# Mixing matmuls as two 64x64 tiles of four blocks in place of four 32x32 tiles of two, with homes of 13 tiles in eleven regions

## The chip, the cores and the metric

The kernel runs on one core of one Trainium2 chip. The metric is device time in microseconds (us); a version's time is the median of its runs. Names of engines: PE is TensorE (PEld its weight loads), DVE VectorE, ACT ScalarE, POOL GpSimd, SP SyncE, which here only issues DMAs.

## The reference, cut to what matters

The input x has shape (1, 16, 1024, 1024): 16 channels, 1024 rows t, 1024 columns s, all float32 (64 MiB in, 64 MiB out). Two layers follow each other.

```python
# layer 0: a bias that depends on the distance row - column, through a small MLP
rel = tril(row - column);  pos = max(rel.max(-1), threshold)
nd  = log(|c*rel| + 1) / (log(|c*pos| + 1) + 1e-6)
h   = relu(nd * W1 + b1)                 # 32 hidden units per (row, column)
x   = x + (h @ W2 + b2)                  # 16 channels
# layer 1: mixing of the 16 channels, with weights of the row and weights of the column
ret  = einsum('MTS,MN->NTS', x, w + eye)
ret += rank-2 mixing with qw1[t], qw2[t]  +  rank-2 mixing with kw1[s], kw2[s]
ret += x * qdd[t]  +  x * kdd[s]
```

Layer 1 is thus, at each point, a 16x16 matrix of its row, A[t], plus a 16x16 matrix of its column, B[s], both applied to the 16 channels of y = x + bias.

## The kernel before, in words

**Layout.** The 1024 columns are cut into 8 blocks of 128. The 128 partitions hold 16 channels of 8 blocks, so that one 128x1024 tile in SBUF is 8 rows t of the whole picture (each partition: 8 rows of one channel of one block). There are 128 such tiles of rows. `GS` blocks share a group of partitions; before, GS is 2, so there are `GROUPS` = 4 groups of `GP` = 32 partitions.

**Mixing.** A row's matrix A[t] must be applied to 16 channels of each block of a group at once, so the weights of a group are a GP x GP matrix that holds the 16x16 matrix GS times on its diagonal and zeros elsewhere. PE's array is used as independent square tiles on its diagonal, one for each group: four of 32x32. A row step (`a_rows`, L732) does one tile of 8 rows: for each of 8 rows and each group one matmul of 128 columns, that is 32 matmuls; float32 makes each of them two weight loads and two matmuls in the trace, 64 of each. A column step (`b_columns`, L743) does 8 columns of a block: per column and group one matmul over all rows of a region (REGION_TILES x 8, 120 as a rule), again 64 loads and 64 matmuls. Its 16 steps cover the 128 columns of all blocks.

**Weights.** The matrices are made once and lie in DRAM as `a_mats` and `b_mats`. `mats_b` (all columns, GS x 16 x 128 floats per partition) is loaded once over zeros. For the rows SP loads chunks of 32 rows into `mats_in` (`load_mats_a`, L325, one DMA per group), and POOL spreads 16 rows at a time into `mats_a` (`spread_unit`, L428), multiplying by a mask `own_block` that leaves the values of a partition's own block and zeros in the others: an output of 128 x (16 x GS x 16). `mats_a` holds two such units.

**Regions and homes.** The 128 row tiles are cut into regions, 8 tiles and then eight times 15. SBUF holds three homes of 15 tiles (60 KB per partition each). In region k one home holds y of the region, a second takes the column mixing of the region (`take_b`: ACT L517 and DVE L629 copy it out of PSUM in turn), to which DVE adds the row mixing (`finish_tile`, L639) and from which it is stored; the third receives x of region k+1, to which the bias is added in place. The bias is added one slot behind where x lies.

**Order.** It is written out by hand, the same on every engine. In region k come 16 column steps, then one row step per tile. Between them, at the steps that `bias_step` names (as a rule every second one), comes a bias tile of region k+1: POOL multiplies the table of logarithms by the row scales (`hidden`, L451), ACT applies the relu (L490), PE multiplies by W2 into `bias` (L757, 128x64 weights, columns 512 wide), DVE and ACT (L657, L501) add the result to x. For the first 64 tiles of rows half the columns have a constant bias, so that one `hidden` per tile is enough; the last 64 need two. `hidden` has three buffers, the PSUM tensor `main` two, `bias` two.

**DMAs.** Loads of x (L317) and the stores (L268) go in pieces of 1 to 4 tiles, 8 DMAs each (one per block, 16 partitions, runs of 512 bytes). SP issues all loads, the loads of `mats_in` and half of the stores; ACT issues the other half. Each queue is in order. A load into a home waits for the store of the tiles that lay there (`load_x`). The pieces 0, 1 and 2 of region k+2 are issued in the row steps 7, 10 and 13 of region k, the rest at the start of region k+1, the last piece in its row step 6.

Of the kernel before, what the change touches and what calls it, by code (L numbers as in the profile page):

```python
# [9 lines left out]
S = 1024  # L10
W = 128
BLOCKS = S // W
GS = 2
GROUPS = BLOCKS // GS
GP = H * GS
HID = 32
# [2 lines left out]
COLS = ROWS * W  # L19
COL_TILES = W // ROWS  # L20
BANK = 512
REGION_TILES = (8,) + (15,) * 8
REGIONS = len(REGION_TILES)
FIRST_TILE = [sum(REGION_TILES[:k]) for k in range(REGIONS)]
ALL_TILES = S // ROWS
HALF_TILES = ALL_TILES // 2
HOME_TILES = max(REGION_TILES)
HOMES = 3
STORE_PIECES = {8: (2, 3, 3), 15: (2, 3, 3, 3, 4)}
LAST_STORES = (2, 3, 3, 3, 2, 1, 1)  # L30
LOAD_PIECES = {8: (1, 3, 4), 15: (1, 3, 3, 3, 4, 1)}
PORTIONS = (2, 2)
CHUNK = 32
CHUNK_TILES = CHUNK // ROWS
# [4 lines left out]
UNITS = S // UNIT  # L39
A_UNIT = H * GS * UNIT  # L40
RING = 3
# [12 lines left out]
def build(nc, x, W1, b1, W2, b2, c, L_mult, init_L, qw1, qw2, kw1, kw2, qdd, kdd, w, out):  # L54
# [6 lines left out]
    with ExitStack() as ctx:  # L61
# [3 lines left out]
        def sem(name):  # L65
            return ctx.enter_context(nc.semaphore(name))
# [4 lines left out]
        homes = sb("homes", [P, HOMES * HOME_TILES * COLS])  # L71
        mats_b = sb("mats_b", [P, GS * H * W])

        mats_in = sb("mats_in", [P, A_RING * H * CHUNK])
        mats_a = sb("mats_a", [P, 2 * A_UNIT])
        own_block = sb("own_block", [P, GS])
        hidden = sb("hidden", [P, RING, COLS])
# [61 lines left out]
        y_const_ready = sem("y_const_ready")  # L140
        main_ready = sem("main_ready")
        main_taken = [sem(f"main_taken{i}") for i in range(2)]
        out_done = [sem(f"out_done{i}") for i in range(len(LAST_STORES))]

        def tile_of(k, T):
            return FIRST_TILE[k] + T
# [30 lines left out]
        def bias_step(k, T):  # L177

            return 1 + T * (COL_TILES + REGION_TILES[k] - 3) // (REGION_TILES[k + 1] - 1)

# [34 lines left out]
            return sum(i < len(pieces(r)) for r in range(k + 1))  # L215

        def store_pieces(k):
            return LAST_STORES if k == REGIONS - 1 else STORE_PIECES[REGION_TILES[k]]

        def load_pieces(k):  # L220
            return LOAD_PIECES[REGION_TILES[k]]

# [35 lines left out]
        def of_block(tensor, pitch, b, offset, dims):  # L258
            start = (b // GS) * GP + b % GS
            return bass.AP(tensor, start * pitch + offset, [[GS * pitch, H]] + dims)  # L260
# [38 lines left out]
        def _(sp):  # L299
# [73 lines left out]
            loaded = [3, 5] + [0] * (REGIONS - 2)  # L373
            for k in range(REGIONS):

                while k + 1 < REGIONS and loaded[k + 1] < 5:
                    load_x(k + 1, loaded[k + 1])
                    loaded[k + 1] += 1
                if k == 2:
                    sp.wait_ge(scales_out, DMA)  # L380
                    sp.wait_ge(nd_ready, PART // 2 // ROWS)
                    sp.dma_start(row_scale[:, 0:PART // 2], late_scales[:, 0:PART // 2]).then_inc(scales_in, DMA)
                if k == 4:
                    sp.wait_ge(nd_ready, PART // ROWS)
                    sp.dma_start(row_scale[:, PART // 2:], late_scales[:, PART // 2:]).then_inc(scales_in, DMA)
                for T in range(REGION_TILES[k]):
                    v = chunk_behind(tile_of(k, T))
                    if v is not None:
                        load_mats_a(v)
                    if k + 1 < REGIONS and T == min(6, REGION_TILES[k] - 4):  # L390
                        load_x(k + 1, 5)
                    for i in range(len(store_pieces(k))):
                        if T == piece_start(store_pieces(k), i + 1) - 1 - (i == 4 and k < REGIONS - 1):
                            store_upper(k, i)
                    if k + 2 < REGIONS and T in (7, 10, 13):
                        load_x(k + 2, loaded[k + 2])
                        loaded[k + 2] += 1
            for i in range(len(out_done)):
# [407 lines left out]
```

## Time and profile before

| | us |
|---|---|
| median of 3 runs | 914.26 |
| lowest and highest run | 906.75, 917.98 |
| profiled execution, span from first to last instruction | 930.2 |
| PE busy with matmuls | 741.4 (80%) |
| DVE, POOL, ACT busy | 452.3, 432.9, 387.6 |
| HBM bytes read, written | 77.61 MB, 69.47 MB |

The profiled execution is one execution; the page gives its span and no separate time. Busy time of PE is taken from modelled ends of pipelined matmuls. DMA share is the mean share of the time in which the 16 DMA engines had a packet under way.

### The profile page before, as it was taken

To read this page: it belongs to the slowest core of one execution; us is meant where nothing else is said; L and a number is where in the kernel's file an instruction comes from. 1 tells how busy PE (TensorE), PEld (TensorE's weight loads), DVE (VectorE), ACT (ScalarE), POOL (GpSimd) and SP (SyncE) were. 2 spreads that over 40 slices of the span, in tenths; PEclk is the share of its full clock that TensorE was granted. 3 is DMA by queue.
4 is the path that set the end of the run, shared out by engine and by line. 5 is a ranking of instruction groups with operands and counts; after the bars stand their busy time and mean duration, and the time that the engine had idled before them with its cause. 6 is when DMAs were issued, how large, how long until landed. Compare 5 with 4: busy or idle time off the path is not lost. (4 is left out here: it accounts for less than half of the span.)

```text
span 930.2 us, 39085 instructions
## 1 busy us (share of the span) xinstructions
PE 741.4 (80%) x18210; PEld 547.7 (59%) x18210; DVE 452.3 (49%) x483; ACT 387.6 (42%) x412; POOL 432.9 (47%) x267
## 2 busy tenths in 40 slices
PE   0678864798678876898799978999689878897984
PEld 0255654576556655666557745677357645676974
DVE  7496522376345533564346524464336524464352
ACT  3958624553463435543433334344233342341200
POOL 3545421254233432365458745586358753581020
PEclk9888887999999999999999999999899988999997
DMA  6787687658975999587976898488875988589068
GB/s 132 183 172 140 147 180 167 145 100 190 194 180 125 183 184 201 124 183 161 223 156 129 174 181 192 94 172 172 182 162 110 199 178 151 106 176 227 5 155 200
DMA packets 301055, 149.63 MB, mean 161 GB/s; under 512 B 30045, under 2 KB 296669, under 8 KB 300893
## 3 DMA queue, kind: packets, MB, share of 16 engines
q1 hardware_dynamic: 231456, 113.56, 56.9%
q10 hardware_dynamic: 69436, 33.58, 17.0%
q8 instruction: 143, 2.34, 1.1%
q14 instruction: 20, 0.16, 0.1%
HBM read 77.61 MB, written 69.47 MB: 158 GB/s over the span
## 5 line engine op out<-in xcount | busy, mean ns | idle before, releaser
L451 POOL TENSOR_TENSOR hidden<-log_table,row_scale 128x1024 f32<-128x1024 f32 x192 | 365.4, 1917 | 367.4 <-PE bias L757 359.5
L743 PE MATMUL main<-homes,mats_b 32*32 32x120 f32 (+1 forms) x9216 | 286.5, 272 | 119.6 <-issue 83.3
L743 PEld LDWEIGHTS main<-homes,mats_b 32*32 32x32 f32 x9216 | 257.9, 133 | 187.5 <-issue 136.1
L490 ACT ACTIVATE hidden<-hidden,b_col 128x1024 f32<-128x1024 f32 x192 | 220.3, 1149 | 310.3 <-POOL hidden L451 205.1
L732 PEld LDWEIGHTS main<-homes,mats_a 32*32 32x32 f32 x8192 | 238.1, 129 | 78.6 <-issue 54.9
L732 PE MATMUL main<-homes,mats_a 32*32 32x128 f32 x8192 | 258.8, 275 | 23.7 <-issue 23.6
L657 DVE SCALAR_TENSOR_TENSOR homes<-bias,b_col,homes 64x512 f32<-64x512 f32 (+1 forms) x256 | 185.8, 747 | 174.9 <-DMA homes<-in_x 106.5
L757 PE MATMUL bias<-hidden,w_blocks 128*64 128x512 f32 x768 | 207.6, 648 | 17.7 <-DVE b_col L620 8.8
L639 DVE TENSOR_TENSOR homes<-main,homes 128x1024 f32<-128x1024 f32 x128 | 156.8, 1225 | 107.7 <-PE main L732 104.6
L629 DVE COPY homes<-main 128x960 f32<-128x960 f32 x64 | 74.1, 1157 | 179.7 <-PE main L743 179.5
L517 ACT ACTIVATE homes<-main 128x960 f32<-128x960 f32 (+1 forms) x80 | 71.1, 891 | 109.4 <-PE main L743 99.3
L428 POOL TENSOR_TENSOR mats_a<-mats_in,own_block 128x512 f32<-128x512 f32 x64 | 66.5, 1040 | 107.4 <-PE main L732 96.7
L501 ACT ACTIVATE homes<-homes,b_col 64x512 f32<-64x512 f32 x128 | 89.4, 749 | 64.5 <-DMA homes<-in_x 54.1
L757 PEld LDWEIGHTS bias<-hidden,w_blocks 128*64 128x64 f32 x768 | 46.4, 143 | 86.6 <-issue 74.6
L697 PE MATMUL bias<-relu_b,w_blocks 128*64 128x1 f32 x2 | 0.3, 241 | 15.1 <-DVE w_blocks L614 15.1
L290 DVE TENSOR_TENSOR homes<-homes 128x2048 f32<-128x2048 f32 x4 | 10.6, 2698 | 0.1
L697 PEld LDWEIGHTS bias<-relu_b,w_blocks 128*64 128x64 f32 x2 | 0.3, 204 | 15.1 <-issue 15.1
L691 PE MATMUL main<-homes 128*128 128x128 f32 x32 | 6.5, 389 | 3.0 <-DVE homes L594 3.0
L691 PEld LDWEIGHTS main<-homes 128*128 128x128 f32 x32 | 5.9, 206 | 4.8 <-DVE homes L594 3.2
L589 DVE TENSOR_TENSOR homes<-homes 128x2048 f32<-128x2048 f32 x2 | 6.2, 3110 | 0.1
L509 ACT ACTIVATE homes<-main 128x1024 f32<-128x1024 f32 x4 | 4.1, 1025 | 2.1 <-PE main L691 2.1
L473 ACT ACT_TABLE_LOAD x1 | 1.3, 1283 | 7.5 <-issue 7.5
(37 smaller groups left out, 32.2 us busy)
## 6 DMA issues: line engine op xcount, KB each, us to landing
homes<-in_x SPq DMA_DIRECT2D x200, 192.0 KB, 6.5
out_mixed<-homes ACTq DMA_DIRECT2D x104, 192.0 KB, 5.9
out_mixed<-homes SPq DMA_DIRECT2D x104, 192.0 KB, 5.6
homes<-in_x SPq DMA_DIRECT2D x72, 256.0 KB, 7.1
homes<-in_x SPq DMA_DIRECT2D x136, 64.0 KB
mats_in<-a_mats SPq DMA_DIRECT2D x128, 64.0 KB
out_mixed<-homes ACTq DMA_DIRECT2D x28, 256.0 KB, 8.0
out_mixed<-homes SPq DMA_DIRECT2D x28, 256.0 KB, 5.8
```

The costliest lines, as they stand in the source:

```text
L428: nc.gpsimd.tensor_tensor(mats_a[:, w % 2 * A_UNIT:(w % 2 + 1) * A_UNIT].rearrange("p (n b e) -> p n b e", n=H, b=GS), rows.unsqueeze(2).t ...
L451: nc.gpsimd.tensor_tensor(hidden_tile(u, g).rearrange("p (j s) -> p j s", j=ROWS), bass.AP(logs.tensor, logs.offset, [list(logs.ap[0]), [1 ...
L490: nc.scalar.activation(hidden_tile(u, g), hidden_tile(u, g), ACT.Relu, bias=b1_col[:, 0:1])\
L501: add = nc.scalar.activation(y_rows(high_half, k, T, b), x_rows(high_half, k, T, b), ACT.Identity, bias=b2_col[high_half, 1:2])
L517: nc.scalar.activation(mixed_columns(k, C), column_sums(k, C), ACT.Copy)\
L629: dve.tensor_copy(mixed_columns(k, C), column_sums(k, C)).then_inc(main_taken[b_tile(k, C) % 2], 1)
L639: dve.tensor_tensor(at, main[:, i % 2, :], at, ALU.add).then_inc(main_taken[i % 2], 1)
L657: add = dve.scalar_tensor_tensor(out=y_rows(rows, k, T, b), in0=falling(u, b, 0 if both else b * (P // 2), P if both else P // 2), scalar= ...
L691: mm = pe.transpose(main[:, i % 2, b * P:(b + 1) * P], comp[part][:, at:at + P], ident)
L732: mm = pe.matmul(main[of_group(g), i % 2, j * W:(j + 1) * W], a_weights(g, w, part * ROWS + j), y_row(k, T, g, j), start=True, stop=True)
L743: mm = pe.matmul(main[of_group(g), i % 2, j * W:j * W + REGION_TILES[k] * ROWS], b_weights(g, C * ROWS + j), y_column(k, g, C * ROWS + j), ...
L757: mm = pe.matmul(bias[into, u % 2, b * BANK:(b + 1) * BANK], w2_blocks[:, g, :], rows, start=True, stop=True)
```

## The change

`GS` becomes 4: a group is four blocks on 64 partitions, and the weights are 64x64 with four 16x16 matrices on the diagonal. There are two groups, so two tiles of 64x64 in the array. `mats_b` grows from 16 to 32 KB per partition, `mats_a` from 4 to 8 KB; for this the homes shrink from 15 to 13 tiles (180 to 156 KB for three), and the regions become 6, nine times 13, and 5 tiles. The pieces of loads and stores, the steps at which SP loads ahead, and the regions at which the late scales are loaded are adapted.

```diff
--- before.py
+++ after.py
@@ -10,7 +10,7 @@
 S = 1024
 W = 128
 BLOCKS = S // W
-GS = 2
+GS = 4
 GROUPS = BLOCKS // GS
 GP = H * GS
 HID = 32
@@ -19,16 +19,17 @@
 COLS = ROWS * W
 COL_TILES = W // ROWS
 BANK = 512
-REGION_TILES = (8,) + (15,) * 8
+REGION_TILES = (6,) + (13,) * 9 + (5,)
 REGIONS = len(REGION_TILES)
 FIRST_TILE = [sum(REGION_TILES[:k]) for k in range(REGIONS)]
 ALL_TILES = S // ROWS
 HALF_TILES = ALL_TILES // 2
 HOME_TILES = max(REGION_TILES)
 HOMES = 3
-STORE_PIECES = {8: (2, 3, 3), 15: (2, 3, 3, 3, 4)}
-LAST_STORES = (2, 3, 3, 3, 2, 1, 1)
-LOAD_PIECES = {8: (1, 3, 4), 15: (1, 3, 3, 3, 4, 1)}
+STORE_PIECES = {6: (2, 2, 2), 13: (2, 3, 3, 3, 2), 5: (2, 1, 1, 1)}
+STORE_SEMS = max(len(sizes) for sizes in STORE_PIECES.values())
+LOAD_PIECES = {6: (1, 2, 3), 13: (1, 3, 3, 3, 2, 1), 5: (1, 4)}
+AHEAD = (7, 10, 12)
 PORTIONS = (2, 2)
 CHUNK = 32
 CHUNK_TILES = CHUNK // ROWS
@@ -140,7 +141,7 @@
         y_const_ready = sem("y_const_ready")
         main_ready = sem("main_ready")
         main_taken = [sem(f"main_taken{i}") for i in range(2)]
-        out_done = [sem(f"out_done{i}") for i in range(len(LAST_STORES))]
+        out_done = [sem(f"out_done{i}") for i in range(STORE_SEMS)]
 
         def tile_of(k, T):
             return FIRST_TILE[k] + T
@@ -215,7 +216,7 @@
             return sum(i < len(pieces(r)) for r in range(k + 1))
 
         def store_pieces(k):
-            return LAST_STORES if k == REGIONS - 1 else STORE_PIECES[REGION_TILES[k]]
+            return STORE_PIECES[REGION_TILES[k]]
 
         def load_pieces(k):
             return LOAD_PIECES[REGION_TILES[k]]
@@ -373,26 +374,27 @@
             loaded = [3, 5] + [0] * (REGIONS - 2)
             for k in range(REGIONS):
 
-                while k + 1 < REGIONS and loaded[k + 1] < 5:
+                while k + 1 < REGIONS and loaded[k + 1] < min(5, len(load_pieces(k + 1))):
                     load_x(k + 1, loaded[k + 1])
                     loaded[k + 1] += 1
-                if k == 2:
+                if k == 3:
                     sp.wait_ge(scales_out, DMA)
                     sp.wait_ge(nd_ready, PART // 2 // ROWS)
                     sp.dma_start(row_scale[:, 0:PART // 2], late_scales[:, 0:PART // 2]).then_inc(scales_in, DMA)
-                if k == 4:
+                if k == 5:
                     sp.wait_ge(nd_ready, PART // ROWS)
                     sp.dma_start(row_scale[:, PART // 2:], late_scales[:, PART // 2:]).then_inc(scales_in, DMA)
                 for T in range(REGION_TILES[k]):
                     v = chunk_behind(tile_of(k, T))
                     if v is not None:
                         load_mats_a(v)
-                    if k + 1 < REGIONS and T == min(6, REGION_TILES[k] - 4):
+                    if k + 1 < REGIONS and len(load_pieces(k + 1)) > 5 and T == min(6, REGION_TILES[k] - 4):
                         load_x(k + 1, 5)
                     for i in range(len(store_pieces(k))):
                         if T == piece_start(store_pieces(k), i + 1) - 1 - (i == 4 and k < REGIONS - 1):
                             store_upper(k, i)
-                    if k + 2 < REGIONS and T in (7, 10, 13):
+                    if k + 2 < REGIONS and (T in AHEAD or k == 0 and T == REGION_TILES[0] - 1) \
+                            and loaded[k + 2] < len(load_pieces(k + 2)):
                         load_x(k + 2, loaded[k + 2])
                         loaded[k + 2] += 1
             for i in range(len(out_done)):
```

## Rows read from the trace of the kernel before

**Rows 1.** The page: PE's total; the instruction DMA queue; DMA packets.
```profile
PE 741.4 (80%) x18210; PEld 547.7 (59%) x18210; DVE 452.3 (49%) x483; ACT 387.6 (42%) x412; POOL 432.9 (47%) x267
...
DMA packets 301055, 149.63 MB, mean 161 GB/s; under 512 B 30045, under 2 KB 296669, under 8 KB 300893
...
q8 instruction: 143, 2.34, 1.1%
```

**Rows 2.** Waits of PE: line, what ended them, us, times, longest.
```profile
PE main L743 <- issue: 83.3, 45, 4.7
PE main L732 <- issue: 23.6, 17, 2.8
PE main L743 <- ACT homes L517: 19.7, 6, 8.6
```

**Rows 3.** Timeline, PE, last region, rows: start, us, what, [idle before, releaser].
```profile
894.95 3.94 PE L732 MATMUL main<-homes,mats_a 32*32 32x128 f32 x127 [1.40 <-issue]
...
905.36 3.85 PE L732 MATMUL main<-homes,mats_a 32*32 32x128 f32 x127 [1.11 <-issue]
912.05 5.45 PE L732 MATMUL main<-homes,mats_a 32*32 32x128 f32 x127 [2.85 <-issue]
918.28 2.28 PE L732 MATMUL main<-homes,mats_a 32*32 32x128 f32 x72 [0.78 <-issue]
```

**Rows 4.** Timeline, PE: undisturbed step pairs and bias tiles, three stretches.
```profile
257.43 1.08 PE L757 MATMUL bias<-hidden,w_blocks 128*64 128x512 f32 x4
258.44 3.59 PE L743 MATMUL main<-homes,mats_b 32*32 32x120 f32 x128
261.96 1.08 PE L757 MATMUL bias<-hidden,w_blocks 128*64 128x512 f32 x4
...
293.34 3.85 PE L732 MATMUL main<-homes,mats_a 32*32 32x128 f32 x128
297.13 1.08 PE L757 MATMUL bias<-hidden,w_blocks 128*64 128x512 f32 x4
...
605.35 3.85 PE L732 MATMUL main<-homes,mats_a 32*32 32x128 f32 x128
609.14 1.94 PE L757 MATMUL bias<-hidden,w_blocks 128*64 128x512 f32 x8
611.01 1.25 PE L732 MATMUL main<-homes,mats_a 32*32 32x128 f32 x36
```

**Rows 5.** Timeline, weight loads of one column step of the first region.
```profile
57.66 0.99 PEld L743 LDWEIGHTS main<-homes,mats_b 32*32 32x32 f32 x64 [0.81 <-issue]
```

**Rows 6.** Windows: stretch, busy us and count per engine, PEclk, DMA share, GB/s.
```profile
0.00:127.80 127.80, 75.49 (x1662) 47.54 (x1662) 81.79 (x89) 79.60 (x98) 59.95 (x43) 0.86 0.72 157
127.80:847.00 719.20, 604.79 (x14564) 441.63 (x14568) 341.60 (x371) 300.19 (x307) 366.73 (x218) 0.95 0.78 164
847.00:930.20 83.20, 61.15 (x1996) 58.53 (x1985) 28.86 (x24) 7.77 (x8) 6.24 (x6) 0.89 0.60 136
333.20:386.50 53.30, 39.75 (x1068) 30.30 (x1060) 20.39 (x23) 27.19 (x31) 14.62 (x9) 0.97 0.88 186
594.00:599.00 5.00, 5.00 (x136) 4.09 (x136) 3.67 (x4) 2.15 (x2) 4.69 (x3) 1.00 0.01 3
624.00:629.00 5.00, 5.00 (x123) 3.44 (x116) 3.24 (x4) 2.30 (x2) 4.16 (x4) 1.00 0.95 247
```

**Rows 7.** Timeline, POOL, row steps of the second half.
```profile
605.50 3.77 POOL L451 TENSOR_TENSOR hidden<-log_table,row_scale 128x1024 f32<-128x1024 f32 x2 [0.72 <-PE bias L757]
609.39 1.04 POOL L428 TENSOR_TENSOR mats_a<-mats_in,own_block 128x512 f32<-128x512 f32 x1
```

**Rows 8.** Timeline, SP's DMA issues; DVE's wait for x.
```profile
640.11 14.87 SPq L317 DMA_DIRECT2D homes<-in_x  x8
...
661.05 28.30 SPq L317 DMA_DIRECT2D homes<-in_x  x24
...
660.69 1.41 DVE L657 SCALAR_TENSOR_TENSOR homes<-bias,b_col,homes 128x512 f32<-128x512 f32 x2 [14.80 <-DMA homes<-in_x]
```

## The prediction, made before the changed kernel had run

> **What bounds the kernel now.** I read the busy shares first, then PE's waits, then PE's timeline around the longest waits, and last the DMA windows stretch by stretch. PE is the busiest engine at 80% [rows 1]; of its idle time, 83.3 + 23.6 = 106.9 us in 62 pieces ends with "issue", that is with nothing the profile shows, against 19.7 us for the largest named wait inside the mixing [rows 2]. The reader should look at where these pieces stand. In the last region, where nothing runs between the row steps, each gap (1.40, 1.11, 2.85, 0.78 us) comes after exactly 127 recorded matmuls; with the equal number of weight loads and a lost record these are 256 PE instructions [rows 3]. 
>
> The DMA engines are the second resource. Over the seven full regions (127.8 to 847 us) they move 164 GB/s at a share of 0.78; the fullest long stretch is 186 GB/s at 0.88, five microseconds reach 247, and at the turn from column to row steps they stand at 3 GB/s for 5 us, since the homes are full until rows are finished [rows 6]. In the column steps x does come late: DVE once waits 14.80 us, while SP needs 14.87 us to issue 8 DMAs and 28.30 us for 24, where its queue is held up by traffic [rows 8].
>
> **PE's stream does not get faster.** A step has 64 matmuls in 32x32 now, four at a time: a pair of row steps takes 297.13 - 293.34 = 3.79 us, a pair of column steps 261.96 - 258.44 = 3.52 [rows 4]. That is 16 rounds of four per step, 118 ns a round with 128 columns and 110 ns with 120, drain at the end included. With two tiles of 64x64 each partition still sees all its columns once per round, so a round costs the same and holds two matmuls instead of four. That two such tiles run side by side is not in the trace; nearest are the bias matmuls, two column halves of 64: 8 of them take 611.01 - 609.14 = 1.87 us [rows 4], 0.23 us each for 512 columns, against about 0.47 if they ran one by one by four times the 118 ns of 128 columns. The bounds are a round at no extra cost and a round twice as long (a rival below); I take no extra cost, since both neighbours, 32x32 and the bias, run side by side.
>
> The loads get twice as wide (64 columns). In the first region, with matmuls of 64 columns, 64 loads of 32 columns go through in 0.99 us, 62 ns for a round of four [rows 5], so 128 loaded columns need at most 62 ns, below the 98 ns of the shortest usual round to come. I take nothing. The Trainium skill (TensorE: Matmul & The Clock Gate, LDWEIGHTS) gives a load as its columns over 1.2 per ns, 107 ns for the 128 columns of a round. By it column steps would grow by 9 ns x 16 x 144 = 21 us. The measured 62 ns contradicts it.
>
> **Part by part, against the span of 930.2 us.**
> - *Column steps.* Per pair 3.52 us at 120 columns becomes about 3.52 x 104/120 = 3.05 to 3.15 (the drain does not shrink); 9 regions of it and two short ones (48 and 40 columns, about 0.75 us a step by the 0.99 us of 64 columns) make 72 x 3.1 + 32 x 0.75 = 247 us, against 64 x 3.52 + 16 x 0.99 = 241 before. +6 us.
> - *Row steps, bias tiles, DVE's and ACT's additions:* same count and size. The copies out of PSUM become 176 smaller ones instead of 144 for the same elements; ACT and DVE are under half busy [rows 1], no cost.
> - *PE's instructions.* Mixing falls from 17408 pairs to 128 x 32 + 176 x 32 = 9728, to 80 packets in all. A packet now lasts four steps, 7 to 7.6 us, plus two bias tiles (1.0 us each in the first half, 1.87 in the second): 9 to 11 us instead of 4.5 to 5.7 [rows 4]. A fetch that made PE wait up to 4.9 us after these 4.5 to 5.7 took at most about 10. So nearly all gaps go: -107 us; -122 if the 0.24 us by which a matmul's modelled end overlaps each gap is counted. Upper bound of the cost left: half of it, if each fetch waits as long as before beside busier data queues. I take -115.
> - *POOL.* The spread unit has 1024 outputs per partition instead of 512: 1.04 us becomes 2.08. In the second half's row steps POOL does 3.77 + 1.04 us in a cycle of 5.66 us (605.35 to 611.01) [rows 4, 7]; now 3.77 + 2.08 = 5.85, 0.2 us over. Regions of 13 put a bias tile after every 2.17 steps, which stretches PE's cycle to about 6. Between 0 and 0.4 us for some 32 cycles: +5 us.
> - *SP and ACT queues.* Loads in 472 DMAs instead of 408, stores 416 instead of 360, chunks of row matrices 64 (twice as large) instead of 128: on SP about 10 more in 740. Bytes stay. No cost of their own.
> - *Start.* Region 0 has two tiles less, region 1 too. About 3 MB less is moved before region 1 begins, of 157 GB/s x 127.8 us = 20 MB [rows 6]: 109 us instead of 127.8, with the work moved behind it.
>
> PE alone would then end near 930 - 115 + 6 + 5 = 826 us. But now the DMAs set the pace. A region of 15 moves 164 x 719.2 / 7 = 16.85 MB, one of 13 moves 14.6. PE needs for it 24 + 24.5 us of steps and 13 bias tiles: 62 us in the first half, 73 to 76 in the second. At the 186 GB/s of the fullest long stretch the DMAs need 78 us, at 175 GB/s 83. Six turns become ten, each with its idle 5 us, but smaller homes hold less ahead. I take 180 GB/s, 81 us, for regions 1 to 8. Region 9 only has 5 bias tiles to make: 24 + 24.5 + 9.4 = 58 us of PE, 60 with waits. Region 10: 16 short steps and 5 rows, 21 us. After the last row 930.2 - 920.6 = 9.6 us of stores remain [rows 3]. Sum: 109 + 8 x 81 + 60 + 21 + 10 = 848 us of span. Of the 115 us some 22 are thus given back as waits for x.
>
> The median of the runs shown, 914.26, is 0.983 of this span; 848 x 0.983 = 833 us.
>
> **Rivals.**
> 1. *The DMAs keep up.* For it: five microseconds reach 247 GB/s, and late x has been partly a matter of SP's order. Against it: no whole region had more than about 175. At 200 GB/s the first half is 73 us a region, the second is set by PE and POOL at 76: 109 + 3 x 73 + 5 x 76 + 91 = 799, times 0.983: 785 us.
> 2. *Fetches get slower as the data queues fill,* and half the gaps stay, on top of the DMA's waits: 848 + 40 = 888, times 0.983: 873 us.
> 3. *The gaps are not fetches,* and stay whatever the count. For it: no row names the cause. Then 930 + 6 + 5 and little else: 941, times 0.983: 925 us. The count of 256 speaks against it. The Trainium skill (Runtime: NRT & Kernel Launch, Instruction fetch mechanics) says that a program is streamed in blocks of 16 KiB and that crossing one is "mostly hidden"; the block size agrees with the rows, "mostly hidden" does not, with 62 gaps in 143 packets.
> 4. *Two 64x64 tiles do not run side by side* (or their loads do not hide), and it gets slower. A full run has (128 + 144) x 16 = 4350 rounds. From 115 / 4350 = 26 ns more per round on the gain is gone; at twice the round, 110 ns more, it is +480 us, PE alone 1300 us. For it: the trace has no 64x64. Against it: both neighbours overlap.
>
> **Chances.** Forecast 0.56 (815 to 860), rival 1 0.18, rival 2 0.12, rival 3 0.08, rival 4 0.06. The range 785 to 880 takes in rivals 1 and 2 and leaves out the last two and little more. What differs by under 2% (896 to 933 us) cannot be told from no change: faster by over 2% 0.86, within 0.08, slower 0.06.
>
> **What would show it.** Right: some 80 instruction packets, "issue" before L743 and L732 under 20 us in all, a clean pair of row steps still near 3.8 us with x64, L428 near 2.08 us, regions of 78 to 84 us at 175 to 185 GB/s, and DVE's waits for x above their present sum. Wrong: row pairs far over 3.8 us (rival 4), gaps of the same sum at other counts (rival 3), regions near 73 us in the first half (rival 1).

## The result: 927 us, 1.6% slower than before, and the profile after

The changed kernel takes 927.11 us (median of 4 runs, 925.63 to 932.32) against 914.17 for the kernel before on the same chip, a ratio of 1.016 (95% interval 1.010 to 1.022). The forecast was 833 us. The span profiled is 925.8 us. From the page: PE, the instruction queue, and the groups of column matmuls and of POOL's spreading; the last line is the group of column matmuls on the page of the kernel before.

```profile
PE 792.2 (86%) x10530; PEld 626.6 (68%) x10530; DVE 455.4 (49%) x499; ACT 394.2 (43%) x428; POOL 485.5 (52%) x267
...
q8 instruction: 83, 1.36, 0.6%
...
L745 PE MATMUL main<-homes,mats_b 64*64 64x104 f32 (+2 forms) x5632 | 354.3, 286 | 90.8 <-ACT homes L519 38.6
...
L430 POOL TENSOR_TENSOR mats_a<-mats_in,own_block 128x1024 f32<-128x1024 f32 x64 | 121.1, 1893 | 59.6 <-PE main L734 58.2
...
L743 PE MATMUL main<-homes,mats_b 32*32 32x120 f32 (+1 forms) x9216 | 286.5, 272 | 119.6 <-issue 83.3
```

Against [rows 1], PE executes 42% fewer matmuls (10530 for 18210) and is busy for 51 us *more*. The packets fell from 143 to 83 as forecast. The column matmuls (L745) alone are busy 354.3 us in 5632 records; the same group before had 286.5 us in 9216.

The waits of PE (line, what ended them, us in total, times, longest):

```profile
PE main L745 <- ACT homes L519: 38.6, 14, 8.5
PE main L745 <- DVE homes L631: 31.8, 5, 7.6
PE main L745 <- DVE homes L659: 15.1, 4, 9.8
```

No matmul waits for "issue" any more: the 106.9 us of [rows 2] are gone. But waits behind the engines that make homes ready and empty PSUM are 85.5 us in place of 36.2 (19.7 + 8.6 + 7.9 in the kernel before). The timeline shows one of them (start, us, what, idle before):

```profile
549.42 1.41 DVE L659 SCALAR_TENSOR_TENSOR homes<-bias,b_col,homes 128x512 f32<-128x512 f32 x2 [5.79 <-DMA homes<-in_x]
...
550.22 5.55 SPq L318 DMA_DIRECT2D homes<-in_x  x8
...
559.75 20.86 SPq L318 DMA_DIRECT2D homes<-in_x  x24
562.45 1.41 DVE L659 SCALAR_TENSOR_TENSOR homes<-bias,b_col,homes 128x512 f32<-128x512 f32 x2 [10.69 <-DMA homes<-in_x]
...
564.84 3.04 PE L745 MATMUL main<-homes,mats_b 64*64 64x104 f32 x32 [7.21 <-DVE homes L631]
...
575.93 3.60 PEld L745 LDWEIGHTS main<-homes,mats_b 64*64 64x64 f32 x64 [0.81 <-issue]
575.93 3.77 PE L745 MATMUL main<-homes,mats_b 64*64 64x104 f32 x64
...
579.63 1.94 PE L759 MATMUL bias<-hidden,w_blocks 128*64 128x512 f32 x8
...
593.44 1.89 POOL L430 TENSOR_TENSOR mats_a<-mats_in,own_block 128x1024 f32<-128x1024 f32 x1 [0.16 <-PE main L734]
595.09 3.91 PE L734 MATMUL main<-homes,mats_a 64*64 64x128 f32 x64
...
598.93 1.51 PE L759 MATMUL bias<-hidden,w_blocks 128*64 128x512 f32 x6
```

Three things are to be seen. At 562.45 DVE has waited 10.69 us for x; the next column step needs a PSUM buffer that DVE must copy out after that, so PE stands 7.21 us behind it. The waits of the list above are nearly all of this kind: the releaser named is DVE or ACT, but 82 of the 85.5 us belong to waits during which, or less than 1 us ahead of which, DVE or ACT ended a wait of its own for x. DVE's waits for x are 158.8 us in all, against 106.5 before. Next, a clean pair of row steps takes 598.93 - 595.09 = 3.84 us, as forecast, while a pair of column steps takes 579.63 - 575.93 = 3.70: with 104 columns it is no faster than with 120 [rows 4], where 3.05 to 3.15 were forecast. Its 32 rounds of weight loads alone take 3.60 us. And a wait costs more than its length: the column step right behind it (564.84) takes 567.81 - 564.84 = 2.97 us, where one of 32 matmuls otherwise takes about 1.9, and the granted clock there is 0.60 (windows below).

The windows (stretch, length, busy us and count of PE, PEld, DVE, ACT and POOL, granted clock, DMA share, GB/s) of regions 1 to 8 as a whole, of two turns from columns to rows with the late x between them, and of the last region's short column steps:

```profile
118.50:804.70 686.20, 615.24 (x8072) 480.15 (x8074) 340.61 (x376) 301.39 (x317) 401.27 (x213) 0.94 0.72 169
500.00:505.00 5.00, 5.00 (x72) 3.98 (x70) 2.76 (x4) 2.33 (x3) 3.79 (x2) 1.00 0.00 0
505.00:510.00 5.00, 5.00 (x72) 3.90 (x68) 3.56 (x4) 1.88 (x2) 3.50 (x2) 1.00 0.01 3
515.00:520.00 5.00, 5.00 (x64) 3.49 (x62) 3.15 (x5) 1.58 (x3) 4.91 (x4) 1.00 1.00 244
560.00:565.00 5.00, 0.16 (x2) 0.16 (x4) 2.55 (x4) 0.71 (x1) 0.00 (x0) 0.71 0.73 156
565.00:570.00 5.00, 5.00 (x40) 3.22 (x40) 2.13 (x3) 0.00 (x0) 0.00 (x0) 0.60 0.97 229
585.00:590.00 5.00, 4.73 (x57) 3.08 (x55) 1.44 (x2) 2.38 (x3) 0.93 (x2) 1.00 0.00 0
590.00:595.00 5.00, 5.00 (x66) 3.58 (x62) 3.25 (x4) 2.30 (x2) 4.84 (x3) 1.00 0.02 3
879.00:903.00 24.00, 24.00 (x440) 24.00 (x438) 2.95 (x6) 3.06 (x7) 0.00 (x0) 0.51 0.15 41
```

These turns leave the DMAs idle for 10 us, not 5. In windows of 1 us over regions 1 to 8 they move less than 20 GB/s in 102 of 686 us, 13 us for each of eight turns; over the seven full regions of the kernel before it was 70 of 719 us, so 10 us a turn there too, which the 5-us window of [rows 6] did not show. When not idle they reach a mean of 198 GB/s (182 before). So the DMAs got faster and the standing still ate it: 169 GB/s over the eight regions, 85.8 us a region instead of 81.

### The profile page after: what moved, and what is told of

Its sections match the earlier page's. It is cut to its first block and busy times, and to the rows that moved or that the text cites. A ratio compares the mean times of both kernels' runs of the same rounds, so it can differ in the third digit from the quotient of the medians.

```text
span 925.8 us, 23815 instructions
## 1 busy us (share of the span) xinstructions
PE 792.2 (86%) x10530; PEld 626.6 (68%) x10530; DVE 455.4 (49%) x499; ACT 394.2 (43%) x428; POOL 485.5 (52%) x267
## 5 line engine op out<-in xcount | busy, mean ns | idle before, releaser
L745 PEld LDWEIGHTS main<-homes,mats_b 64*64 64x64 f32 x5632 | 338.4, 203 | 152.8 <-issue 55.1
L745 PE MATMUL main<-homes,mats_b 64*64 64x104 f32 (+2 forms) x5632 | 354.3, 286 | 90.8 <-ACT homes L519 38.6
L659 DVE SCALAR_TENSOR_TENSOR homes<-bias,b_col,homes 64x512 f32<-64x512 f32 (+1 forms) x256 | 185.9, 747 | 244.6 <-DMA homes<-in_x 158.8
L734 PEld LDWEIGHTS main<-homes,mats_a 64*64 64x64 f32 x4096 | 239.9, 184 | 44.6 <-issue 34.9
L734 PE MATMUL main<-homes,mats_a 64*64 64x128 f32 x4096 | 251.6, 276 | 0.0
L759 PE MATMUL bias<-hidden,w_blocks 128*64 128x512 f32 x768 | 200.2, 629 | 13.8 <-DVE b_col L622 8.7
L430 POOL TENSOR_TENSOR mats_a<-mats_in,own_block 128x1024 f32<-128x1024 f32 x64 | 121.1, 1893 | 59.6 <-PE main L734 58.2
L631 DVE COPY homes<-main 128x832 f32<-128x832 f32 (+1 forms) x80 | 77.6, 970 | 137.5 <-PE main L745 137.3
L519 ACT ACTIVATE homes<-main 128x832 f32<-128x832 f32 (+2 forms) x96 | 73.0, 760 | 115.9 <-PE main L745 110.9
L291 DVE TENSOR_TENSOR homes<-homes 128x2048 f32<-128x2048 f32 x4 | 10.6, 2694 | 0.1
L486 ACT ACTIVATE mats_b<-zero_col 128x8192 f32<-128x8192 f32 x1 | 7.0, 7013 | 0.0
(37 smaller groups left out, 30.6 us busy)
```

The lines of the kernel that those rows point to most:

```text
L430: nc.gpsimd.tensor_tensor(mats_a[:, w % 2 * A_UNIT:(w % 2 + 1) * A_UNIT].rearrange("p (n b e) -> p n b e", n=H, b=GS), rows.unsqueeze(2).t ...
L519: nc.scalar.activation(mixed_columns(k, C), column_sums(k, C), ACT.Copy)\
L631: dve.tensor_copy(mixed_columns(k, C), column_sums(k, C)).then_inc(main_taken[b_tile(k, C) % 2], 1)
L659: add = dve.scalar_tensor_tensor(out=y_rows(rows, k, T, b), in0=falling(u, b, 0 if both else b * (P // 2), P if both else P // 2), scalar= ...
L734: mm = pe.matmul(main[of_group(g), i % 2, j * W:(j + 1) * W], a_weights(g, w, part * ROWS + j), y_row(k, T, g, j), start=True, stop=True)
L745: mm = pe.matmul(main[of_group(g), i % 2, j * W:j * W + REGION_TILES[k] * ROWS], b_weights(g, C * ROWS + j), y_column(k, g, C * ROWS + j), ...
```

## The experiments

**1. Rounds of matmuls alone.** PE runs series of rounds without any data transfer: 32x32 and 64x64 tiles, several numbers of columns.

```
for _ in range(64):  # 64x64, 2 tiles, 64 columns
    for row in (0, 64):
        pe.matmul(into[row:row + 64, 0:64], stationary(row, 64, 64, 1), moving[row:row + 64, 0:64], ...)
```

> A kernel of its own that leaves out the whole computation: thirteen series of float32 matmuls on constant data, no DMA traffic, tiles on the diagonal of the array. Read is the time from one matmul of a tile to the next of the same tile (a round). In the changed kernel a round of two 64x64 tiles takes 109 to 110 ns with 40, 48 and 104 columns alike, where 34 to 93 ns were expected from the columns. Theory A (the load of a tile's weights sets a floor of about 1.7 ns per weight column, each tile for itself, side by side): 64x64 tiles 109 ns with 16 to 64 columns whether one tile or two are used, and with stride 1 as with stride 128; 32x32 tiles about 55 ns with one, two or four tiles; 64 rows x 32 columns about 55 ns, 32 rows x 64 columns 109 ns. Theory B (the loads of all tiles go one after the other through one port, 55 ns for 64 columns): one 64x64 tile about 55 ns, two 109 ns; 32x32 tiles 27, 55 and 109 ns for one, two and four. Theory C (the scattered weights are the reason, stride 128 in the column weights): stride 1 shows rounds well under 109 ns, and only stride 128 shows 109 ns. With 128 columns all theories give 113 ns.

PE's timeline:

```profile
26.58 1.99 PE L53 MATMUL into<-moving,weights 32*32 32x64 f32 x128 [0.68 <-issue]
30.58 1.99 PE L53 MATMUL into<-moving,weights 32*32 32x64 f32 x128 [2.02 <-issue]
34.31 1.99 PE L53 MATMUL into<-moving,weights 32*32 32x64 f32 x128 [1.74 <-issue]
...
78.59 7.63 PE L62 MATMUL into<-moving,weights 64*64 64x64 f32 x256
86.05 16.48 PE L65 MATMUL into<-moving,weights 64*64 64x16 f32 x384
102.37 20.64 PE L68 MATMUL into<-moving,weights 64*64 64x20 f32 x192
122.94 10.37 PE L71 MATMUL into<-moving,weights 32*32 32x20 f32 x191
...
133.17 10.44 PE L74 MATMUL into<-moving,weights 32*32 32x24 f32 x383
```

An f32 matmul of the code shows as two records, so L62 has 128 rounds of two 64x64 tiles, in 86.05 - 78.59 = 7.46 us, 58 ns each with 64 columns. So such a round can be as short as its columns: wide loads as such are not the reason for 110 ns. From L65 on the granted clock falls (0.60 at 90 to 95 us) to 0.50 (the 1.2 GHz level), which spoils the comparison by columns; but there one 64x64 tile (L68) takes 20.57/192 = 107 ns a load, one 32x32 tile (L71) 53 and two of them (L74) 54. So the loads of tiles on the diagonal go side by side; one after another is refuted. The run shows one thing more: with the DMAs idle, 32x32 rounds still stop after every 128 matmuls, every 3.7 to 4.0 us (26.58, 30.58, 34.31).

**2. What else differs: the stride.** In the row steps (L734) a matrix's weights lie side by side; in the column steps (L745) they lie 128 floats apart. This run changes the stride from one series to the next, and nothing else in the series shown here, 96 rounds of two records with 64 columns each (stride 1 against stride 128, cut):

```
-    pe.matmul(into[row:row + 64, 0:64], stationary(row, 64, 64, 1), ...)
+    pe.matmul(into[row:row + 64, 0:64], stationary(row, 64, 64, 128), ...)
```

> A kernel of its own that leaves out the whole computation: series of 48 rounds of float32 matmuls on constant data, a run of 32 dense rounds with 128 columns before each so that the clock is up. Two 64x64 tiles with 64 columns and weights read at a stride of 1, 2, 4, 8, 16, 32, 64 and 128 floats; four 32x32 tiles with 48 columns at strides 1, 16 and 128; two 64x64 tiles with 104 columns at stride 128, and one such tile alone with 64. Theory C (weights read at a wide stride load at 1.7 ns a column, 110 ns for 64, whatever the clock; contiguous ones at half of it or less): stride 1 at 57 to 59 ns, stride 128 at 109 to 111 ns with 64 and with 104 columns, one tile or two; 32x32 at 43 ns with stride 1 and 56 with stride 128. Where between 2 and 128 it turns is open. Theory A (the floor belongs to 64 weight columns, and the one series at 58 ns was something else): all strides at 109 ns.

PE's timeline; L53, L59, L65, L71, L77 and L95 have stride 1, 2, 4, 8, 16 and 128:

```profile
20.20 5.76 PE L53 MATMUL into<-moving,weights 64*64 64x64 f32 x192
25.80 7.15 PE L56 MATMUL into<-moving,weights 64*64 64x128 f32 x128
32.79 5.92 PE L59 MATMUL into<-moving,weights 64*64 64x64 f32 x192
...
45.53 11.62 PE L65 MATMUL into<-moving,weights 64*64 64x64 f32 x192
...
63.98 11.63 PE L71 MATMUL into<-moving,weights 64*64 64x64 f32 x192
...
82.44 10.82 PE L77 MATMUL into<-moving,weights 64*64 64x64 f32 x192
...
135.18 10.77 PE L95 MATMUL into<-moving,weights 64*64 64x64 f32 x192
```

From start to next start: 58 ns a round at stride 1, 60 at 2, 120 at 4 and 8, 111 at 16, 110 at 128; one tile alone takes 111 too, 104 columns 113. Four 32x32 tiles with 48 columns take 43 ns contiguous and 58 at stride 16 or 128. So a load whose weights lie 4 floats or more apart costs 1.7 to 1.9 ns per weight column, with 64 columns and with 104: the 58 ns of 32 columns hid under 120 columns before, 110 does not hide under 104. In the changed kernel itself a round of 104, 48 or 40 columns takes 110 ns in the median.

**3. The column matrices made contiguous.** POOL spreads them from a compact copy at the start, in place of zeros and DMAs, so that 64 weights lie side by side (cut to the line that reads them).

```
-    return bass.AP(mats_b, GP * g * GP * W + col, [[GP * W, GP], [W, GP]])
+    return bass.AP(mats_b, GP * g * GP * W + col * GP, [[GP * W, GP], [1, GP]])
```

> The changed kernel with the column weights laid out so that the 64 weights of a column are contiguous: mats_b is filled once by POOL from a compact copy (four operations at the start) in place of zeros and DMAs at stride 128. Nothing else. Theory C: column rounds fall from 110 to about 90 ns with 104 columns and to about 58 ns or less with 40 and 48; 18 ns x 16 x 144 = 41 us and about 25 us less of PE in the column steps, of which part comes back as waits for x; 870 to 900 us. Rival (loads of 64 columns have a floor of 110 ns in this kernel in any layout): within 10 us of the changed kernel, 917 to 937 us.

910.53 us (904.91 to 914.35), ratio 1.004 (0.9997 to 1.008). The page's line of busy times:

```profile
PE 739.9 (81%) x10530; PEld 570.8 (63%) x10530; DVE 466.0 (51%) x499; ACT 386.1 (42%) x427; POOL 505.4 (55%) x271
```

PE's timeline at a pair of column steps:

```profile
571.10 3.10 PE L759 MATMUL main<-homes,mats_b 64*64 64x104 f32 x64
```

The waits of PE that rose:

```profile
PE main L759 <- ACT homes L533: 55.5, 20, 9.2
PE main L759 <- DVE homes L645: 42.1, 9, 8.7
PE main L759 <- DVE homes L673: 15.2, 4, 9.3
```

The column pair takes the 3.10 us forecast. PE is busy 52 us less, and the time falls by 17 only (by 11 if the ratios to the kernel before, 1.016 and 1.004, are compared), short of the 870 to 900 expected: the waits behind ACT and DVE rise from 85.5 to 112.8 us, of which 98 again go with a wait of theirs for x. The stride was real, and it was not all: most of what mending it gives is lost again to late x.

**4. The regions alone.** The changed kernel with 32x32 tiles, `GS = 4` put back to `GS = 2`:

> Only the regions and homes of the change (6, nine times 13, 5 tiles), with the mixing of before: groups of two blocks, four 32x32 tiles. Theory A (the change lost on the floor of its column rounds and on late x, and gained the gaps between instruction packets): here column rounds go with 104 columns at 88 to 92 ns, PE's instructions rise to 2 x 20200 or so, the issue gaps are there again (110 to 135 us), and there are two more turns between regions; 925 to 950 us, L428 back at 1.04 us. Rival (the regions of 13 tiles alone explain the loss, the 64x64 mixing in itself gains 100 us as predicted): over 1000 us.

989.52 us (981.97 to 998.44), against 908.64 for the kernel before beside it, ratio 1.092 (1.083 to 1.102): between the two expected ranges. PE's waits:

```profile
PE main L745 <- issue: 84.4, 48, 6.4
PE main L745 <- DVE homes L631: 35.6, 5, 11.0
PE main L745 <- ACT homes L519: 27.6, 11, 12.4
PE main L734 <- issue: 15.3, 12, 3.6
...
PE main L745 <- DVE homes L659: 12.7, 4, 8.9
```

The trace is of the slowest of the four runs (998.4 us). The gaps are as large as before (99.7 against 106.9 us), the waits behind ACT and DVE twice as large (75.9 against 36.2), PE is busy 22 us more with 2048 more matmul records. So homes of 13 tiles, with their pieces and load steps, cost 9.2%, some 84 of 914 us, and the 64x64 mixing brings the ratio back from 1.092 to 1.016, some 69 us (62 between the two medians, which are of different chips). The change is two changes with opposite signs.

**5. In between, homes of 14.** 32x32 tiles, one region of 7, eight of 14, one of 9:

```
-REGION_TILES = (8,) + (15,) * 8
+REGION_TILES = (7,) + (14,) * 8 + (9,)
```

> The mixing of before (groups of two, 32x32 tiles) with homes of 14 tiles: regions of 7, eight times 14, and 9 tiles, ten regions where before had nine and the change eleven; pieces and steps of the loads as before. Theory A (each further turn costs, since the DMA engines stand still there for 10 us and the first x comes late behind it, and each further region adds 16 column steps): half way from 911 to 990 us, 935 to 965 us. Rival (what cost 79 us with regions of 13 is in the places of pieces and loads chosen for 13): within 12 us of the kernel before.

962.87 us (950.04 to 964.51), ratio 1.049 (1.038 to 1.060), as expected. With 15, 14 and 13 tiles (nine, ten, eleven regions) the ratio goes 1, 1.049, 1.092, the waits behind ACT and DVE 36, 62, 76 us, the time in which the DMAs stand still (windows of 1 us below 20 GB/s, from the start of region 1 to that of the last) 70, 102, 135 us, or 10, 13, 15 us a turn.

**6. The traffic taken away.** Only a quarter of the finished rows are stored: of the changed kernel, of the kernel before, and of experiment 3's kernel.

```
-            return eng.dma_start(out[0, :, t0:t0 + n, ...], home_rows(b, mixed_slot(k, T), n))
+            q = n // 4
+            return eng.dma_start(out[0, :, t0:t0 + q, ...], home_rows(b, mixed_slot(k, T), q))
```

> The changed kernel with a quarter of the rows of each stored piece actually stored (three quarters of the output are left out); same number of DMAs, same waits. DMA bytes fall by about a third. Theory A (what holds the column steps up beside the load floor is the x that comes late behind full DMA engines): PE's waits behind ACT's and DVE's evictions fall from 85 us to under 30, regions of 13 go from 88 to about 80 us, total 850 to 875 us. Rival (the waits come from somewhere else, POOL or the order of the steps): total stays over 900 us.

> The kernel before with a quarter of the rows of each stored piece actually stored (three quarters of the output are left out); same PE instructions, same number of DMAs. Theory (PE's issue gaps are packets of its program that wait behind data in the DMA engines): the gaps fall from 107 us in 62 pieces to under 60 us, and those that stay come in the column steps, where the loads of x are; total 840 to 870 us. Rival (the gaps belong to PE's instruction count alone, not to the data traffic): still 95 us or more.

> The changed kernel with contiguous column weights, and only a quarter of the rows of each stored piece stored (three quarters of the output are left out). It has neither the load floor nor full DMA engines. Theory A (both together are what the prediction lacked): PE's waits behind evictions under 40 us, total 785 to 820 us, where the contiguous weights alone gave 910 and the quarter stores alone 856. Rival (a third cost, POOL's longer spread or the turns themselves): over 835 us.

855.98, 851.21 and 830.47 us (one run each): the first two as expected, the third between its ranges. In the first, PE's waits behind ACT and DVE ahead of column steps fall from 85.5 to 31.6 us (under 30 was expected), so most of them come from the traffic. PE's longest waits, in the kernel before with a quarter stored:

```profile
PE main L744 <- issue: 51.2, 35, 4.8
PE main L744 <- ACT homes L518: 24.3, 7, 8.4
```

and with contiguous 64x64 tiles and a quarter stored:

```profile
PE main L760 <- ACT homes L534: 38.2, 15, 8.4
```

When only data traffic is taken away the gaps of the kernel before fall from 106.9 + 1.5 us (the latter ahead of bias tiles) to 51.2 + 3.5 + 6.2 = 61: they depend on the traffic, as fetches through the same DMA engines would, and by experiment 1 some would be there without any. In spans, the changed kernel gets shorter by 925.8 - 854.1 = 72 us, the contiguous one by 912.5 - 828.7 = 84. But the kernel before gains from the same cut too. Each set against the kernel before beside it, the cut is worth 59 us there, 68 in the changed kernel and 85 in the contiguous one, so only some 9 and 25 us of it belong to the change. And with the traffic cut the changed kernel is still no faster than the kernel before: it has none of the 61 us of gaps, but PE is busy 777.9 us against 718.9. With contiguous weights PE is busy 718.9 us as well, and the time is 21 us shorter.

**7. The order of the loads.** The loads of the region after next stand in SP's queue behind row steps 7, 10 and 12. Put earlier:

```
-AHEAD = (7, 10, 12)
+AHEAD = (4, 7, 10)
```

first in the changed kernel, then in experiment 3's.

> The changed kernel with one line different: SP issues the first three pieces of x of the region after next in the row steps 4, 7 and 10 of a region, not 7, 10 and 12. Theory A (x comes late in the column steps because of the order on SP's queue; the DMA engines stand still for some 12 us at each turn and are full after it): the first pieces land before they are wanted, PE's waits behind the evictions (85 us in all in the changed kernel) fall by 25 to 50 us, 880 to 905 us. Rival (the DMA engines are full in the second part of the row steps, so another order moves only which transfer is late): within 8 us of the changed kernel, 919 to 935 us.

> The contiguous column weights and the loads of x in row steps 4, 7 and 10 together. Theory C with late x as the second cause: the 12 us that the earlier loads gave alone come on top or grow, as PE now waits for x more often; 855 to 885 us, clearly below the kernel before. Rival (with PE faster the DMA engines are the bound and order is worth nothing): same as the contiguous weights alone within 5 us.

915.4 us (913.11 to 925.45, ratio 1.015, 1.006 to 1.024) and 889.47 (888.74 to 890.84, ratio 0.976, 0.970 to 0.983): by medians 12 and 21 us less, the first between the two expected ranges, the second just above the first theory's. By the ratios it is 1 us (1.016 to 1.015) and 26 us, so the first gain is not shown by the times alone; PE's waits behind ACT and DVE did fall there, from 85.5 to 70.6 us. In the second PE's longest wait is now

```profile
PE main L759 <- DVE homes L673: 52.8, 9, 9.6
```

L673 adds the bias to x and waited for the last piece of the next region. That piece is taken ahead of the others:

```
-    if k + 1 < REGIONS and len(load_pieces(k + 1)) > 5 and T == min(6, REGION_TILES[k] - 4):
+    if k + 1 < REGIONS and len(load_pieces(k + 1)) > 5 and T == min(4, REGION_TILES[k] - 4):
```

> Contiguous column weights and early loads as in the kernel with both, and one thing more: the last piece of the next region's x (one tile, wanted by the bias tile of row step 11) is issued in row step 4, ahead of the other region's first piece, and not in row step 6. In the trace of the kernel with both, DVE waits 7.4 us for this piece in the row steps. Theory A (what holds PE up is which transfer stands first on SP's queue): that wait goes at some of the nine turns, PE's waits behind DVE (52.8 us) fall by 15 to 40 us, 855 to 882 us. Rival (the DMA engines are full there and the wait moves to the first pieces in the column steps): within 6 us of 889 us.

> As the kernel with the last piece in row step 4, but the first pieces of the region after next in row steps 5, 8 and 10 in place of 4, 7 and 10, so that the last piece and the stores have the queue to themselves for longer. Theory A: between 855 and 885 us; within 8 us of the other one either way, better if the last piece was still late there, worse if the first pieces are.

885.37 us (883.9 to 890.41) with the other loads at 4, 7, 10, and 882.47 (875.4 to 884.17; ratio 0.972, 0.959 to 0.985) with them at 5, 8, 10. In the first of the two:

```profile
PE main L759 <- ACT homes L533: 56.6, 20, 10.4
...
PE main L759 <- DVE homes L673: 9.6, 1, 9.6
```

The wait aimed at fell from 52.8 to 9.6 us and the time by 4, which is what the rival expected (within 6 us of 889): other waits grew (behind L533 from 37.4 to 56.6, behind L645 from 0.5 to 12.2), and the sum of the three only fell from 90.7 to 78.4. Order moves a wait; only what it shortens in sum counts.

**8. Stores off SP's queue.** SP and ACT each issue half of a store; ACT now more, `PORTIONS = (2, 2)` to `(3, 3)`.

> The kernel with contiguous column weights, the last piece in row step 4 and first pieces in row steps 5, 8 and 10 (882 us), with one constant changed: ACT issues the stores of six of the eight blocks, three and three, and SP of two. Theory A (SP's queue is too full, and the loads stand behind its stores): x is issued about 1.3 us earlier per piece, 865 to 880 us. Rival (the DMA engines, not the queue that issues, are the bound, and ACT now comes later to its relu): 880 to 900 us.

881.57 us (880.59 to 882.17), 0.9 less than without it, which is within the scatter of both and in the rival's range (880 to 900): nothing shows SP's queue as such to be the bound. It has the lowest median, ratio 0.966 (0.962 to 0.970) to the kernel before. Its waits behind ACT and DVE are still 52.7 + 10.6 + 9.9 = 73 us, of which 58 go with a wait of theirs for x.

**9. The order in the kernel before.** First with its loads later (behind row steps 9, 12, 14 in place of 7, 10, 13), then with the last piece at 4 and the others at 5, 8, 11.

> The kernel before, with its own mixing and homes of 15 tiles, where SP issues the first three pieces of x of the region after next in row steps 9, 12 and 14 of 15 in place of 7, 10 and 13: as near to the end of the region as the change has them (7, 10, 12 of 13), 6, 3 and 1 steps before the turn in place of 8, 5 and 2. Theory A (the smaller homes cost time because x is asked for that much nearer to the turn): PE's waits behind the evictions (36 us) grow by 20 to 50 us, 925 to 955 us. Rival (the number of turns costs the time, not the lead of the loads): within 10 us of the kernel before.

> The kernel before with the same new order on SP's queue: last piece in row step 4 in place of 6, first pieces of the region after next in row steps 5, 8 and 11 in place of 7, 10 and 13. Theory A (in the kernel before, the gaps between packets of PE's program hide most of the late x, so order is worth little): 895 to 915 us. Rival (order is worth as much here as in the changed kernel, and the 64x64 tiles brought nothing): 875 to 892 us.

914.28 us (ratio 0.997, 0.989 to 1.004) and 904.12 (885.85 to 916.16; ratio 0.977, 0.968 to 0.987). Later loads change nothing, as the rival expected, so the lead with which a load stands in the queue was not what the kernel before lived on. The second order, within the 895 to 915 expected, may help it too, by 1% (medians) to 2% (the ratio given): two of its four runs (911 and 916 us) are no faster than the kernel before, the other two (897 and 886) are. So how much of experiment 8's 3.4% is owed to the 64x64 mixing and how much to the order is not settled.

## Why the prediction was wrong

The ladder in medians, with the ratio to the kernel before beside it: before 914 (1), homes of 13 tiles 990 (1.092), 64x64 tiles 927 (1.016), contiguous weights 911 (1.004), order 882 (0.972). By the forecast's own phases, the span came out as 118.5 + 686.2 + 69.3 + 39.7 + 12 = 926 against 109 + 648 + 60 + 21 + 10 = 848.

PE's own account of the two profiled spans closes. From 930.2 to 925.8 us: gaps ahead of "issue" -108, PE busy +51, waits behind ACT and DVE ahead of column steps +49, the rest +4. With contiguous weights, from 930.2 to 912.5: gaps -108, busy -1, waits +77, the rest +15 (8.6 of it for POOL's spreading at the start). The forecast had -115 for the gaps, +6 for column steps, +5 for POOL and +22 for the waits. The execution profiled of the kernel before was a long one, so these spans differ by less than the medians do.

**Right: the gaps.** Packets 83 for 80, "issue" 0 for "under 20 us"; rival 3 falls with experiment 6 too. Rival 2 (slower fetches) did not come: no matmul waited for a packet once a packet lasted 9 us and more.

**Right: "a round costs the same" in the row steps,** 3.84 us for 3.79, and tiles side by side (rival 4's main part). POOL's spreading took 1.89 us for 2.08, and the row steps show no wait for it.

**Wrong: "The loads get twice as wide ... I take nothing".** The 62 ns came from a 64-column round of 32x32 tiles [rows 5], that is from loads half as wide; I scaled them by the 128 columns loaded in all, as if tiles shared one load path. They load side by side, and each takes 1.7 to 1.8 ns a column at this stride: 58 ns then, 110 now. Rival 4's bracket, "or their loads do not hide", is what happened, at 20 ns a round of the column steps only. In the page's reckoning, which gives the kernel before 286.5 us where the forecast counted 241, the column steps grew by 68 us where +6 was forecast, and with contiguous weights (299.7) by 13. So the loads cost PE 55 us; in time, mending them was worth 11 to 17.

The Trainium skill (TensorE: Matmul & The Clock Gate, LDWEIGHTS) has columns over 1.2 per ns. Read per tile, 64 columns, it gives 53 ns. The trace of experiment 2 does not contradict it for contiguous weights: a round of 64 columns takes 58 ns there, little more than half of the 109 that one of 128 columns takes between them (32.79 - 25.80 = 6.99 us for 64 rounds), so the load took 58 ns at most. Strided ones take twice the 53. The prediction read it over all 128 columns of a round; its 107 ns comes near the measured 110 for a reason that experiment 1 refutes.

**Wrong: the last region, "about 0.75 us a step".** It took 39.7 us for 21. Its 16 column steps of 40 columns ran at a granted clock of 0.51, the 1.2 GHz level, two steps in 3.65 us. Contiguous weights did not help there (experiment 3's last column phase took 30.6 us, 4.5 of them waits, for 29.2): its clock was at 0.50 too, and at that level a round with contiguous weights takes 107 ns in it, one with strided weights 110. The 0.99 us that I took were read in the first region of the kernel before, at a granted clock of 0.89 around it.

**Wrong, and the main error: "Of the 115 us some 22 are thus given back as waits for x".** PE's waits behind the engines that wait for x rose by 49 us, and by 77 in experiment 3, where the loads hide as the forecast had it; that kernel's span is still 64 us over the forecast 848. The term behind it is "Six turns become ten, each with its idle 5 us, but smaller homes hold less ahead. I take 180 GB/s": I named the effect and gave it no price. The count was wrong as well: nine regions became eleven. A turn stood still for 10 us in the kernel before and for 13 to 14 in the changed one, 122 us from region 1 to the last, for the 50 that ten turns of 5 make; at unchanged mixing homes of 14 and 13 raised it from 70 to 102 and 135 us, and the time by 4.9 and 9.2%, some 45 and 84 us. The rate came out as 169 GB/s, a region as 85.8 us for 81. A rival in which the smaller homes cost more than the gaps give back was missing from the list; experiment 4's two numbers for it, +84 and -69 us, are in no row of before. What does it, the number of turns, the size of a home, or the pieces and load steps chosen for it, was not separated: all change together in 4 and 5. Experiment 9 only shows that later loads cost nothing with homes of 15.

"PE alone would then end near 826 us" lies close to the 828.7 of experiment 6, but I don't count it as confirmed: that kernel has contiguous weights, its column matmuls are busy for 282 us instead of 247, and a quarter of the stores still runs.

**Wrong: the factor 0.983.** It was this one profiled execution of the kernel before that ran 1.7% over its median. Later profiles lie nearer to their kernels' medians as a rule (925.8 to 927.1, 912.5 to 910.5, 996.6 to 989.5), but one of experiment 9 is 1.2% under its own (903.5 to 914.3). 848 us would have been the forecast; 15 of the 94 us missed are this.

## What to carry to other kernels

A gap in the busiest engine is often the cover of the next resource's lateness: before its removal is counted as a gain, ask what the engine would wait for next, and price a smaller buffer by the time in which the DMAs stand still. Price a change of tile shape and a change of buffer size each alone: here they were about -69 and +84 us. And when weights are read with a stride, check the load against the shortest matmul it must hide under, per tile and not for all tiles together.

## What the runs showed of the hardware that I had not expected

- Weights 4 or more floats apart load in 109 to 120 ns for 64 columns at full clock, contiguous or 2 apart in at most 58 to 60; 4 and 8 apart (120 ns) are slower than 16 to 128 apart (109 to 111).
- At the 1.2 GHz level a load of 64 contiguous columns shows as 107 ns, of 32 as 53 (one tile) or 54 (two). Strided loads of 64 columns take 110 ns at either level: in the changed kernel's rounds of 40 and 48 columns the median is 110 ns at both.
- After a long wait of PE the granted clock is at the 1.2 GHz level for some us: 0.71 and 0.60 in the two windows around the 7.21 us of the example, with a column step of 2.97 us in place of 1.9.
- Series of matmuls with 16 to 24 columns ran at a granted clock of 0.5 although PE was busy throughout, and so did the last region's steps of 40 columns at 0.50 and 0.51; the steps of 104 and 128 columns in the windows above ran at 1.00.
- With no data traffic a packet of 256 PE instructions comes every 3.7 to 4.0 us (experiment 1), and series of rounds that execute one in 2 us stand still between them.
